# Moving the shared expert and the second expert rows behind the last two attention heads, in a four-layer fp32 kernel on one core

## The reference

```
xn = _layernorm(x)
x = x + _L1_attn_ref(xn, wq, wk, wv, wo)          # 16 heads of 128, window of 128 keys
      + _L1_ffn_ref(xn, ...)
# _L1_ffn_ref:
shared_sum = _ffn(flat_x, shared_w1, shared_w2)    # h = x@w1; (x1 * silu(x2)) @ w2, all 1024 tokens
routed: 7 experts, each takes its 146 best tokens; every token has at most two experts
out = _ffn(flat_x[sel_idx], routed_w1, routed_w2)
routed_sum = zeros.at[sel_idx].add(out * w)
return shared_sum + routed_sum
xn = _layernorm(x)                                 # layer 2 begins
```

## Time and profile before

| what | value |
|---|---|
| median of three runs | 762.70 us |
| profiled execution / its span | 763.62 us / 761.5 us |
| TensorE (PE) busy | 668.8 us, 88% |
| VectorE (DVE) busy | 539.3 us, 71% |
| GpSimd (POOL) busy | 367.5 us, 48% |
| ScalarE (ACT) busy | 345.1 us, 45% |
| granted TensorE clock over the span | 0.959 of 2.4 GHz |

### The profile page before, as it was taken

One profiled execution on the slowest core, in us unless ns is written; L12 is line 12 of the kernel. 1 busy time (PEld: TensorE's weight loads), 2 busy tenths in 40 slices (PEclk: granted clock), 3 DMA queues, 4 the chain that ended last, 5 costly groups with the idle time before them and its releaser, 6 DMA issues.

```text
span 761.5 us, 11708 instructions
## 1 busy us (share of the span) xinstructions
PE 668.8 (88%) x3944; PEld 513.5 (67%) x3944; DVE 539.3 (71%) x1050; ACT 345.1 (45%) x747; POOL 367.5 (48%) x278
## 2 busy tenths in 40 slices
PE   4799999999789999999999997989897998667557
PEld 1354555578368988889898887979686456455446
DVE  3347577664589889797979974654378637499995
ACT  2275211120345574756565553654355512667440
POOL 0100488700267576574747478693374111546661
PEclk9999999999999999999999999999998999977798
DMA  9500000000510101010000111104212001000001
GB/s 303 227 1 30 28 1 1 2 1 0 184 31 22 35 21 34 21 34 20 31 3 21 35 31 56 35 23 156 77 29 50 1 0 34 1 0 1 0 1 55
DMA packets 14435, 31.15 MB, mean 41 GB/s; under 512 B 1822, under 2 KB 8445, under 8 KB 13759
## 3 DMA queue, kind: packets, MB, share of 16 engines
q1 hardware_dynamic: 12493, 26.33, 10.1%
q0 software_dynamic: 1536, 3.15, 1.5%
q10 hardware_dynamic: 370, 1.18, 0.6%
HBM read 26.46 MB, written 5.24 MB: 42 GB/s over the span
## 4 chain that ended last, share of the span: by engine, by line
PE 50%; DVE 27%; issue 8%; POOL 8%; ACT 3%; DMA 3%; DVEq 1%; SPq 0%; POOLq 0%; ACTq 0%
PE bank L529 8%; PE bank L538 7%; PE bank L548 6%; PE bank L550 5%; PE bank L549 5%; PE bank L714 3%; DVE x L1555 3%; DVE arena L1539 2%; PE bank L744 2%; DVE arena L1530 2%; PE bank L592 2%; PE bank L728 2%; DVE arena L1529 2%; PE bank L743 2%; DVE zone L1768 2%
## 5 line engine op out<-in xcount | busy, mean ns | idle before, releaser
L548 PE MATMUL bank<-zone 128*128 128x256 f32 (+1 forms) x408 | 143.8, 352 | 19.6 <-DVE arena L1530 5.0
L550 PE MATMUL bank<-zone 128*128 128x256 f32 (+1 forms) x408 | 133.2, 326 | 0.0
L549 PE MATMUL bank<-zone 128*128 128x256 f32 (+1 forms) x408 | 133.0, 326 | 0.0
L1916 POOL TENSOR_TENSOR arena<-arena 128x512 f32<-128x512 f32 x64 | 82.2, 1285 | 71.8 <-ACT arena L1153 71.8
L548 PEld LDWEIGHTS bank<-zone 128*128 128x128 f32 x408 | 78.8, 193 | 36.2 <-DVE arena L1530 10.6
L1921 POOL TENSOR_TENSOR arena<-arena 128x512 f32<-128x512 f32 x64 | 83.2, 1300 | 29.0 <-DVE arena L1530 19.8
L550 PEld LDWEIGHTS bank<-zone 128*128 128x128 f32 x408 | 78.8, 193 | 6.4
L549 PEld LDWEIGHTS bank<-zone 128*128 128x128 f32 x408 | 79.0, 194 | 4.3
L529 PE MATMUL bank<-xT,arena 128*128 128x512 f32 x160 | 77.3, 622 | 2.1 <-ACT xT L1042 0.8
L1172 ACT ACTIVATE arena<-arena 128x256 f32<-128x256 f32 (+1 forms) x128 | 62.0, 487 | 32.5 <-DVE arena L1539 32.4
L1555 DVE SCALAR_TENSOR_TENSOR x<-bank,arena,x 128x256 f32<-128x256 f32 x128 | 52.7, 470 | 18.3 <-PE bank L550 18.3
(11 more groups left out here) (296 smaller groups left out, 1419.5 us busy)
## 6 DMA issues: line engine op xcount, KB each, us to landing
arena<-in_qk SPq DMA_DIRECT2D x16, 256.0 KB, 2.8
arena<-in_tern SPq DMA_DIRECT2D x1, 3072.0 KB, 21.7
arena<-in_wv SPq DMA_DIRECT2D x8, 256.0 KB, 2.7
arena<-in_wo SPq DMA_DIRECT2D x16, 128.0 KB, 2.1
arena<-in_wr SPq DMA_DIRECT2D x1, 1792.0 KB, 11.4
lB<-in_lB SPq DMA_DIRECT2D x1, 1288.5 KB, 24.2
arena<-in_lA SPq DMA_DIRECT2D x1, 1282.5 KB, 15.1
x<-in_x SPq DMA_DIRECT2D x1, 1024.0 KB, 12.7
```

Source lines behind the costliest of these rows:

```text
L548: pe.matmul(dst, lhi, rhi, start=(n == 0), stop=False)
L549: pe.matmul(dst, lhi, rlo, start=False, stop=False)
L550: last = pe.matmul(dst, llo, rhi, start=False, stop=(n == len(terms) - 1 and not open_end))
L1916: pool.tensor_tensor(qraw[:, j, :], qraw[:, j, :], cosT[:, at], ALU.mult).then_inc(cos_done, 1)
```

## The change

Nothing is computed differently. The order changes:

- TensorE: `shared_in` and `shared_out` stand behind head 15, and no longer ahead of head 14. What frees the banks for head 14 is now the routed experts' results, no longer the shared expert's.
- ScalarE: the rounded copies of the shared weights (L1233, L1236) stand behind the last `keep_y`, and no longer between the experts; the shared expert's SiLU and copies stand behind head 15.
- VectorE: the shared expert's products and remainders stand behind head 15. All second rows are added after them, then each pair of the shared expert's result is added, measured and, per block, normalised. The first rows keep their place.
- POOL: four fetches, then `turn_qk` steps 0 and 1, four fetches, `rest_of_wo(14)`, `turn_qk` steps 2 and 3, then all eight second-row fetches, then `rest_of_wo(15)`.

```diff
@@ tensor
-            shared_in()
-            shared_out()
             for left in HEAD1["left"]:
                 pe.wait_ge(*left)
             head(H1 // 2 - 1, 0, True, True, HEAD1)
             head(H1 // 2 - 1, 1, False, False, HEAD1)
+            shared_in()
+            shared_out()
@@ scalar
-                if e == 0:
-                    act.wait_ge(w1s_loaded, 16)
-                    act.activation(w1s2[0].bitcast(F32R), w1s, ACT.Copy).then_inc(w1s_hi, 1)
-                if e == 1:
-                    act.wait_ge(w2s_loaded, 16)
-                    act.activation(w2s2[0].bitcast(F32R), w2s, ACT.Copy).then_inc(w2s_hi, 1)
             keep_y(ER - 1)
+            act.wait_ge(w1s_loaded, 16)
+            act.activation(w1s2[0].bitcast(F32R), w1s, ACT.Copy).then_inc(w1s_hi, 1)
+            act.wait_ge(w2s_loaded, 16)
+            act.activation(w2s2[0].bitcast(F32R), w2s, ACT.Copy).then_inc(w2s_hi, 1)
+            head(H1 // 2 - 1, 0, True, False, HEAD1)
+            head(H1 // 2 - 1, 1, False, False, HEAD1)
...
-            head(H1 // 2 - 1, 0, True, False, HEAD1)
-            head(H1 // 2 - 1, 1, False, False, HEAD1)
@@ vector, in head(..., last=True)
                     add_head(h, p, base)
-                    if last:
-                        x_is(4 * h + base["added"] + p + 1)
-                        for t in (2 * p, 2 * p + 1):
-                            add_rows(1, t)
-                        dve.wait_ge(combined, NT + 2 * p + 2)
-                        measure((2 * p, 2 * p + 1))
-                        if p % 2:
-                            normalise(2, xn2, p // 2)
@@ vector, behind the shared expert's products and remainders
+            x_is(4 * H1 + HEAD1["added"])
+            for t in range(NT):
+                add_rows(1, t)
             for p in range(NT // 2):
+                dve.wait_ge(combined, NT + 2 * p + 2)
                 x_is(g_s2[p].ready[1] - 1)
                 add_pair(g_s2[p], p)
-            head(SPLIT, base=HEAD1)
-            head(H1 - 1, more=False, base=HEAD1, last=True)
+                x_is(g_s2[p].ready[1])
+                measure((2 * p, 2 * p + 1))
+                if p % 2:
+                    normalise(2, xn2, p // 2)
@@ gpsimd
-            fetch_rows(range(0, 6))
-            turn_qk(H1 - 1, (0, 1), HEAD1)
-            rest_of_wo(SPLIT)
-            turn_qk(H1 - 1, (2, 3), HEAD1)
-            fetch_rows(range(6, 2 * NT - 4))
+            fetch_rows(range(0, 4))
+            beside_head(SPLIT, HEAD1, between=lambda: fetch_rows(range(4, 8)))
+            fetch_rows(range(8, 2 * NT))
             rest_of_wo(H1 - 1)
-            fetch_rows(range(2 * NT - 4, 2 * NT))
```

More of the change, by code:

```diff
@@ L406, in build @@
         g_r2 = [group((y_act, y_dve)[e % 2], OUT1[e % 4]) for e in range(ER)]
-        g_s1 = [(group(eprod_ready, 2 * b), group(esilu_ready, 2 * b + 1)) for b in range(NB)]
-        g_s2 = [group(x_added, b) for b in OUT1]
-        HEAD1 = dict(uses=[HEAD0["uses"][b] + uses[b] - before[b] for b in range(8)], added=HEAD0["added"] + len(g_s2), left=list(left_by))
+        HEAD1 = dict(uses=[HEAD0["uses"][b] + uses[b] - before[b] for b in range(8)], added=HEAD0["added"], left=list(left_by))
         for b in range(8):
@@ L414, in build @@
         left_by += [(x_added, counts[x_added] - 3 + OUT1.index(b)) for b in range(4, 8)]
+        g_s1 = [(group(eprod_ready, 2 * b), group(esilu_ready, 2 * b + 1)) for b in range(NB)]
+        g_s2 = [group(x_added, b) for b in OUT1]
         turn[0] = 0
@@ L1627, in head @@
                     if last:
-                        dve.wait_ge(combined, NT + 2 * p)
+                        dve.wait_ge(combined, 2 * p + 2)
                     add_head(h, p, base)
-                    if last:
-                        x_is(4 * h + base["added"] + p + 1)
-                        for t in (2 * p, 2 * p + 1):
-                            add_rows(1, t)
-                        dve.wait_ge(combined, NT + 2 * p + 2)
-                        measure((2 * p, 2 * p + 1))
-                        if p % 2:
-                            normalise(2, xn2, p // 2)
             dve.wait_ge(cs_loaded, 32)
@@ L1695, in _ @@
             dve.tensor_copy(yg[0:LEAD, ER - 2, :], g.ps[0:LEAD, :]).then_inc(g.ready_sem, 1)
+            head(SPLIT, base=HEAD1)
+            head(H1 - 1, more=False, base=HEAD1, last=True)
             for b in range(NB):
```

## The result

| kernel | median, us | ratio to before | 95% interval |
|---|---|---|---|
| before | 763.16 (4 runs, 760.43 to 764.98) | | |
| changed | 775.00 (4 runs, 772.85 to 776.01) | 1.0154 | 1.0116 to 1.0193 |
| changed, measured once more | 770.84 (6 runs, 768.02 to 773.23; before there: 763.18, 25 runs) | 1.0098 | 1.0061 to 1.0135 |

The change makes the kernel slower, by 1.0 to 1.5%. The forecast was 773.7 us, a ratio of 1.0144 to the median of 762.7. The first measurement lies 1.3 us above it, a loss of 11.8 us by the medians; the second gives 7.7 us of loss where 11.0 were forecast. The two intervals overlap.

A forecast was written before the change was run, and what follows sets the result against it. The prediction took the chain of waits, half through TensorE and over a quarter through VectorE, as the bound. First transpose +9.4 us and clock 1.6 gave +11.0: 773.7 us against the median of 762.7, range 768.5 to 778.

The forecast's parts named there:

- Start of head 14: TensorE, banks freed by the routed results: head 14 starts at 537.9, 12.5 us earlier, behind a hole of 1.6 us.
- ScalarE without cover: Ahead of head 14, ScalarE's copies and table load lie uncovered, delaying TensorE's `project_qk` step 2: cost 0.6 us.
- First wait: TensorE at `project_out(14)` stands until POOL's gathers and `rest_of_wo(14)` are done: 4.1 us.
- Second wait: TensorE at `scores(15, 2)` stands for POOL's fourth `qk_ready`: 2.3 us, so head 15 starts at 561.9.
- Third wait: TensorE at `project_out(15)` stands for `rest_of_wo(15)`, behind all eight second-row gathers on POOL: some 2.7 us.
- Clock: Behind the third wait the granted clock falls to half: 1.6 us, bounds 0 and 3.4; other falls lie under waits.
- VectorE's tail: VectorE's second rows, shared pairs and normalising, from the end of `shared_out` to the first transpose: 5.2 us, before 5.4.
- Sum: First transpose of layer 2 at 594.2 instead of 584.84, +9.4 us; with the clock +11.0.
- Rival A: POOL's gathers hold nobody up: first transpose at 585.5, +0.7 us, 763.4, no change; chance 0.09.
- Rival B: A, and no hole lets the clock fall ahead of the gates: -2.3 us, 760.4, faster; chance 0.04.
- Rival C: Half clock also through head 15's start and longer in `project_out(15)` and `shared_in`: adds 2 to 5 us, 776 to 779; chance 0.15.

The follow-up runs named there:

- rows_by_sync: Changed kernel with POOL's 16 gathers replaced by 16 plain DMAs on SyncE's queue, leaving out which row belongs to which token: 761.73 us against 764.41, ratio 0.9984.
- wo14_first: Changed kernel with `rest_of_wo(14)` ahead of gathers 4 to 7 and no longer behind them: 771.15 us, ratio to before 1.0090.
- pool_order_alone: Kernel before, shared expert still ahead of head 14, with POOL's new order and nothing else: 769.27 us, ratio 1.0074.
- pool_freed: Changed kernel, POOL reordered: three gathers, `turn_qk(15)`, `rest_of_wo(14)`, five, `rest_of_wo(15)`, eight; VectorE's first rows behind `add_head(15)`: 763.90 us against 764.41, ratio 1.0002.
- rows_between: pool_freed with the second rows spread over VectorE's idle time, from between the shared expert's two products on: 760.56 us against 763.18, ratio to before 0.9961.
- clock_held: rows_between with a wait before each later ternary turn, meant to spread the four; they did not spread: 758.61 us, ratio to before 0.9950.

## Why the prediction was right

Step by step, in us from the start of the routed stage, so that the 0.66 us of the execution drops out:

- *Start of head 14.* Predicted 12.5 us earlier, measured 12.6 (28.75 to 16.11). The hole is 1.05 us where 1.6 was forecast.
- *ScalarE without cover.* Predicted cost 0.6 us. In rows_by_sync, where POOL does not disturb, head 14 takes 14.2 us to `project_out` instead of 14.0: 0.2. Too dear by 0.4, without effect on the end, since POOL's wait lies over it.
- *First wait.* Predicted 4.1 us, measured 4.07, ended by `rest_of_wo(14)`.
- *Second wait.* Predicted 2.3 us, or less if `project_out(14)` ran at half clock, and head 15 5.5 us ahead of before. Measured 0.59 and 5.7: the clock did fall and, as forecast, it was hidden by this wait. wo14_first, where `project_out(14)` ran at the full clock, shows the first and second waits as one of 6.35 us; 4.1 and 2.3 are 6.4.
- *Third wait.* Predicted 2.7, measured 2.99. `project_out(15)` starts 3.3 us ahead of before (forecast 3.2).
- *Clock.* Predicted 1.6 us in `project_out(15)`. The first profile shows 1.4 (4.39 against 2.95), the repeat none. The forecast's lower bound for this term, no fall, is what the repeat shows. That the term fell due in one execution and not in the other is luck. Its upper bound of 3.4 was too high by the row that it names: eight matmuls of the gates take 3.5 us at the full clock (19 took 8.42 in the kernel before) and took 6.12, so 2.6 more.
- *VectorE's tail.* This term was mis-sized. Eight second rows were put at 0.49 each, from the total of eight first rows beside POOL's gathers in the earlier trace rows, 3.9 us. Measured in the changed kernel:

```profile
586.52 3.25 DVE L1596 SCALAR_TENSOR_TENSOR x<-arena,x 128x256 f32<-128x256 f32 x8
589.69 0.68 DVE L1382 TENSOR_TENSOR x<-x,bank 128x512 f32<-128x512 f32 x1
590.40 0.75 DVE L1366 BATCH_NORM_STATS2 stats<-x 128x6 f32<-128x256 f32 x2
591.07 0.67 DVE L1382 TENSOR_TENSOR x<-x,bank 128x512 f32<-128x512 f32 x1
591.78 0.75 DVE L1366 BATCH_NORM_STATS2 stats<-x 128x6 f32<-128x256 f32 x2
```

  Eight rows take 3.25 us, 0.7 less; the rest of the tail (589.69 to the transpose at 594.87) is 5.2 us against 5.3 forecast. In the earlier trace rows one of the eight had taken 1.22 us, the others 0.48, so that total was not a price for eight (the source line in the kernel before, ns min/median/max):

```profile
L1598 DVE SCALAR_TENSOR_TENSOR x<-xT,arena,x x8: 472/480/1222, 571.5 to 575.0; 128x256 f32<-128x256 f32 x8
```
- *Sum.* First transpose forecast at +9.4 and the clock's 1.6; measured +9.4 with the clock's 1.4 in it, and +7.9 in the repeat. Without the clock the forecast was 1.45 us too dear: 0.38 up to the end of `project_out(15)`, 0.22 up to the second rows, 0.73 in these rows and 0.12 behind them. Behind the transpose the forecast took the distance to block 1's gates as unchanged. The repeat was 1.2 us quicker there, because its transposes ran at the full clock (1.65 us against 2.18 before) and a larger part of block 0's gates did (5.2 us against 6.0). So the waits are as forecast, and the closeness of the total is in part luck: the terms were too dear by 1.45 us, and the first median lies 4.2 us above the second. The forecast ratio of 1.0144 lies inside the first interval and just above the second; beside the repeat the kernel before alone ranged from 759.33 to 768.09 us.
- *Rival A*, the gathers hold nobody up, gave 763.4. rows_by_sync makes that case real: 761.73 against 764.41. By my working its mechanism would have been worth 0.7 us of loss; the run showed a transpose 1.0 us earlier than before. Of these 1.7 us, 1.1 lie behind the start of `shared_in` (0.7 of them the rows), 0.4 are ScalarE's and 0.2 the start of head 14. What head 15 gained up to `project_out(15)` (8.6 us instead of 8.9) was lost in `project_out(15)`, 3.5 us instead of 3.2. The gathers themselves kept the price of the earlier trace rows in the changed kernel: 1.30 us from one to the next.
- *Rival B*, A and a clock that stays up, gave 760.4 by 3.0 us less in block 0's gates. In rows_by_sync they took 5.1 us against 6.0 before: a part of it at most.
- *Rival C*, more of it at half clock, shows in part: the clock fell in `project_out(14)` in both profiles of the changed kernel and at the start of head 15 in wo14_first. Both times a wait for POOL behind it hid the fall, so it did not add the 2 to 5 us.

## What to carry to other kernels

When work moves on one engine, ask what stood beside it on the others. Here the shared expert's 14 us on TensorE had been the cover for gathers on POOL, and its matmuls do not run on POOL at all. The change also gave POOL a new order, and pool_order_alone shows that this order costs 6.1 us even with the cover in its old place. The old order at the new place was not run. An estimate from 1.31 us for a gather, 5.3 us for two steps of `turn_qk` and the times at which TensorE asks for them puts its waits at some 4.7 us, so both parts seem to matter. pool_freed shows that an order made for the new place removes them.

Count an in-order queue's items against the time at which each is asked for. The longest hole in a profile may be worth nothing if the next item in the same queue is as late. Ask also what the moved work is to overlap with: the shared expert was on TensorE's path at both places, and only filling VectorE's idle time behind it (rows_between) paid, 0.4% over the kernel before (interval 0.1% to 0.7%).

## What the runs showed of the hardware

- The granted clock after a hole differs between executions of one program. Behind the hole of 2.17 us ahead of `shared_out` it stayed at 1.00 in the first profile of the changed kernel and fell to 0.50 in the repeat; behind the hole of 2.99 us it was the other way round.
- A hole above 2 us right ahead of the fall is not needed: in clock_held the clock was back at 1.00 after `shared_out` and fell to 0.50 at the start of the gates, with waits of 0.81 and 1.05 us between the ternary turns, the transposes and the gates; in rows_between the same with 0.66 and 1.20 us.
- The recorded times of back-to-back operations of VectorE overlap: each L1596 lasts 0.476 us, and eight take 3.25 us, 0.40 from start to start.
- A gather (an indirect DMA of 128 rows) holds POOL's queue: 1.00 us for itself and 0.30 before the next, 1.30 us from one to the next.
